# One program's order rewritten, and one tile's value products moved into it

## The reference, cut to what matters

```python
x = layernorm(x + L0_attn(x))   # latent attention, 32 heads, causal
x = layernorm(x + L0_ffn(x))    # routed low-rank stage, below
x = layernorm(x + L1_attn(x))   # q, k, v clipped; q and k normalised; ALiBi attention, 32 heads of 16
x = layernorm(x + L1_ffn(x))    # gated feed-forward, 1792 hidden

# L0_ffn: dense product, bias, and one of four low ranks chosen for each token
out = x @ W.T + b
probs = softmax(x @ gate_w.T + gate_b)          # the largest of four wins
final = (x @ A[:r].T @ B[:, :r].T)              # r = 8, 16, 32 or 64, by the winner
```

## Time and profile before

| | us |
|---|---|
| median of three runs | 1512.86 (1512.28 to 1513.26) |
| the profiled execution | 1512.49 |
| its span | 1510.7 |
| TensorE busy | 1422.4 (94%) |
| VectorE busy | 939.8 (62%) |
| ScalarE busy | 813.4 (54%) |
| GpSimd busy | 533.9 (35%) |

### The profile page before, as it was taken

One profiled execution on the slowest core, in us unless ns is written; L12 is line 12 of the kernel. 1 busy time (PEld: TensorE's weight loads), 2 busy tenths in 40 slices (PEclk: granted clock), 3 DMA queues, 4 the chain that ended last, 5 costly groups with the idle time before them and its releaser, 6 DMA issues. The chain is left out here.

```text
span 1510.7 us, 23933 instructions
## 1 busy us (share of the span) xinstructions
PE 1422.4 (94%) x8048; PEld 1011.7 (67%) x8048; DVE 939.8 (62%) x1521; ACT 813.4 (54%) x1731; POOL 533.9 (35%) x495
## 2 busy tenths in 40 slices
PE   5699999999999999999977987999999999999997
PEld 4566776776677777677646874555555558888885
DVE  4455665555566555566668646766666427767967
ACT  3566766666666566666533322565565665333433
POOL 0134454333445443344042134404131024444442
PEclk9799999999999999999989998999999999999998
DMA  5233334333333433332410045534335032000000
GB/s 186 71 47 47 41 50 53 36 48 44 45 41 51 53 35 48 42 40 38 87 56 1 1 56 71 71 44 62 53 53 107 34 118 120 1 0 1 3 25 28
DMA packets 61666, 75.90 MB, mean 50 GB/s; under 512 B 20641, under 2 KB 42145, under 8 KB 60705
## 3 DMA queue, kind: packets, MB, share of 16 engines
q1 hardware_dynamic: 57248, 64.55, 24.6%
q0 software_dynamic: 4352, 10.49, 5.1%
HBM read 42.49 MB, written 2.10 MB: 30 GB/s over the span
## 5 line engine op out<-in xcount | busy, mean ns | idle before, releaser
L1682 DVE TENSOR_REDUCE pm<-l_sm 128x2 f32<-128x1024 f32 (+1 forms) x192 | 178.5, 956 | 96.0 <-PE l_sm L1556 59.9
L1642 ACT ACTIVATE l_probs<-l_banks 128x512 f32<-128x512 f32 (+3 forms) x366 | 165.6, 495 | 134.1 <-PE l_banks L1586 83.0
L666 ACT ACTIVATE probs<-sc,nmax 128x128 f32<-128x128 f32 (+7 forms) x256 | 190.1, 743 | 72.1 <-DVE nmax L750 68.1
L750 DVE TENSOR_REDUCE nmax<-sc 128x1 f32<-128x128 f32 (+7 forms) x256 | 193.5, 756 | 32.6 <-PE sc L493 27.1
L674 ACT COPY pt<-tb 128x512 f32<-128x512 f32 (+3 forms) x256 | 129.3, 505 | 151.1 <-PE tb L507 150.1
L507 PE MATMUL tb<-ident,probs 128*128 128x128 f32 x1152 | 172.5, 275 | 2.1 <-ACT pt L674 1.1
L78 PE MATMUL sc<-k_h,q_h 128*128 128x512 f32 (+4 forms) x384 | 144.4, 376 | 10.5 <-DVE q_l L774 8.7
L507 PEld LDWEIGHTS tb<-ident,probs 128*128 128x128 f32 x1152 | 132.1, 141 | 13.5 <-DVE pt L758 3.8
L1583 PE MATMUL l_banks<-qk_bufs 128*128 128x512 f32 (+3 forms) x366 | 134.8, 410 | 0.8 <-ACT l_probs L1642 0.4
L529 PE MATMUL mb<-pt,ckv 128*64 128x512 f32 (+2 forms) x736 | 131.7, 493 | 3.2 <-DVE x_tok L740 2.9
L78 PE MATMUL sc<-k_h,q_l 128*128 128x512 f32 (+4 forms) x384 | 132.4, 345 | 0.0
(11 more groups left out here) (288 smaller groups left out, 3107.7 us busy)
## 6 DMA issues: line engine op xcount, KB each, us to landing
gated_late<-in_gated SPq DMA_DIRECT2D x11, 768.0 KB, 13.2
wout<-in_w_out SPq DMA_DIRECT2D x16, 512.0 KB, 4.4
late<-late SPq DMA_DIRECT2D x128, 64.0 KB, 2.0
rb<-rT SPq DMA_DIRECT2D x248, 32.0 KB, 4.5
qk_bufs<-late SPq DMA_DIRECT2D x96, 64.0 KB, 5.7
qk_bufs<-late POOLq DMA_DIRECT2D x96, 64.0 KB, 6.7
nope_t<-in_nope_by_dim SPq DMA_DIRECT2D x16, 192.0 KB, 3.9
late<-in_gated SPq DMA_DIRECT2D x3, 768.0 KB, 7.9
```

Source lines behind the costliest of these rows:

```text
L666: act.activation(prob_row(n, s), score_row(n)[0], ACT.Exp, bias=nmax[:, s:s + 1], accum_out=ssum[:, n:n + 1]).then_inc(exped, 1)
L750: dve.tensor_reduce(nmax[:, n % 4:n % 4 + 1], row, axes, ALU.max, negate=True).then_inc(negmax, 1)
L1642: act.activation(probs[(NC * g + c) % RING][:, h, 0:w], e_slot(g, n)[:, 0:w], ACT.Exp).then_inc(exped, 1)
L1682: dve.tensor_reduce(pm[g % 2][:, :, s, i, half], slot(("m", g, n))[:, :, 0:w], AX.X, ALU.max, negate=True).then_inc(freed, 1)
```

## The change

In the latent attention's tail VectorE takes no statistics of tiles 4 to 7; it takes them in the routed program, behind its first four lower halves. In the routed program the order of all four engines is another one, the eight bias additions move from GpSimd to VectorE in three places, and the value products of the last tile are computed there, behind the 16 projections, and copied out by VectorE. The ALiBi program computes 7 tiles of values, with half of the seventh ahead of the score units and half between the first two, and waits for 7. GpSimd there waits for the first maxima before it issues group 1's moves, and loads the constant rows of group 1 before that wait.

```diff
@@ stage_mla, tail_add
-                    dve.wait_ge(tail_read, j + 1)
-                    keep.n1.stats(dve, j, keep.x[:, j, :])
+                    if j < 4:
+                        dve.wait_ge(tail_read, j + 1)
+                        keep.n1.stats(dve, j, keep.x[:, j, :])
@@ stage_front, TensorE
+                def project_v(j):
+                    pe.wait_ge(wqh, 3 * DK)
+                    pe.wait_ge(wql, 3 * DK)
+                    pe.wait_ge(clip, len(order) - 3)
+                    first, rest = split_terms(cols(j), wqkv_h[2], wqkv_l[2])
+                    three(pe, po[0][:], first + rest).then_inc(qkv_ps, 1)
                 down_rank(0)
-                turn_x1(4)
-                turn_x1(5)
                 base(0)
                 back(0)
-                turn_x1(6)
-                turn_x1(7)
+                for j in range(4, ST):
+                    turn_x1(j)
                 base(1)
                 down_rank(1)
                 base(2)
+                back(1)
                 turn_lo(0)
-                back(1)
                 base(3)
-                turn_lo(1)
                 for j in range(4):
                     lora(j)
                 for j in range(4, ST):
                     base(j)
+                    if j == 4:
+                        turn_lo(1)
                     lora(j)
...
+                project_v(ST - 1)
@@ stage_front, ScalarE
                 upper_x(0, 0)
-                n1.root(act, 4, ST, 1)
                 upper_x(1, 1)
...
                 w_copy(3)
+                act.copy(b_hh[:], bT2).then_inc(w_h, 1)
+                n1.root(act, 4, ST, 1)
+                qkv_copy(0, range(2))
                 act.wait_ge(n1.inv_ok, 4)
                 for j in ON_ACT:
...
-                act.copy(b_hh[:], bT2).then_inc(w_h, 1)
                 ag_copy(0)
+                qkv_copy(0, range(2, DK))
                 for j in range(4, ST):
                     upper_x(j, j)
-                qkv_copy(0, range(DK))
-                qkv_copy(1, range(2))
+                qkv_copy(1, range(DK))
                 ag_copy(1)
                 upper_lo(0)
-                qkv_copy(1, range(2, DK))
+                n2.root(act, 0, 1, 0)
+                n2.root(act, 1, 2, 1)
+                normalise(0)
                 upper_lo(1)
-                n2.root(act, 0, 1, 0)
-                for j in range(1, 4):
+                for j in range(2, 4):
                     n2.root(act, j, j + 1, j)
                     normalise(j - 1)
@@ stage_front, VectorE
+                def add_bias(j):
+                    dve.wait_ge(tr_ps, j + 1)
+                    dve.tensor_tensor(keep.x[:, j, :], keep.x[:, j, :], bias, ALU.add).then_inc(biased, 1)
+
+                for j in range(4):
+                    lower_x(j, j)
+                for j in range(4, ST):
+                    n1.stats(dve, j, keep.x[:, j, :])
                 n1.variance(dve, 4, ST)
-                lower_x(0, 0)
                 n1.inverse(dve, 4, ST, 1)
                 dve.wait_ge(n1.inv_ok, 3)
-                lower_x(1, 1)
                 n1.normalise(dve, 4, keep.x[:, 4, :])
-                lower_x(2, 2)
                 n1.normalise(dve, 5, keep.x[:, 5, :])
-                for j in range(3, ST):
+                dve.wait_ge(keep.small_in, 16)
+                for j in range(2):
+                    add_bias(j)
+                for j in range(4, ST):
                     lower_x(j, j)
-                dve.wait_ge(keep.small_in, 16)
                 route(0)
+                for j in range(2, 4):
+                    add_bias(j)
                 lower_lo(0)
                 route(1)
+                add(0)
+                add(1)
+                n2.inverse(dve, 0, 1, 0)
                 lower_lo(1)
-                add(0)
-                for j in range(1, 4):
+                for j in range(2, 4):
                     add(j)
                     n2.inverse(dve, j - 1, j, j - 1)
                 n2.inverse(dve, 3, 4, 3)
+                for j in range(4, ST):
+                    add_bias(j)
...
+                dve.wait_ge(qkv_ps, len(order) + 1)
+                dve.tensor_copy(keep.v[:, ST - 1, :], po[0][:])
@@ stage_front, GpSimd
-                for j in range(ST):
-                    pool.wait_ge(tr_ps, j + 1)
-                    pool.tensor_tensor(keep.x[:, j, :], keep.x[:, j, :], bias, ALU.add).then_inc(biased, 1)
@@ alibi_order
-    order = [... cast ...] + [("v", k, j) for j in range(6) for k in range(DK)]
-    late_v = [("v", k, j) for j in (6, 7) for k in range(DK)]
+    order = [... cast ...] + [("v", k, j) for j in range(V_TILES - 1) for k in range(DK)]
+    late_v = [("v", k, V_TILES - 1) for k in range(DK)]
+    order += late_v[0:2]
     for n in range(M_HALF):
-        order += [("m", 0, n), late_v[n]]
+        order += [("m", 0, n)] + late_v[2 + n:3 + n]
@@ stage_alibi: SyncE before group 1's moves, TensorE before e(0, 0), GpSimd before values(0, 0)
-                wait for ST value tiles
+                wait for V_TILES = ST - 1 value tiles
@@ stage_alibi, GpSimd
-                for b in range(1, BUFS):
-                    pads(b)
-                    load_rows(b)
-                    if b == 1:
-                        move_keys(1)
-                        values(1, 1)
-                        pool.wait_ge(vx_ok, 2)
+                pads(1)
+                load_rows(1)
+                pool.wait_ge(rows_first, ROWS)
+                move_keys(1)
+                values(1, 1)
+                pool.wait_ge(vx_ok, 2)
+                pads(2)
+                load_rows(2)
```

More of the change, by code:

```diff
@@ L1320 @@
 AHEAD = 4
+V_TILES = ST - 1
 def chunk_cols(c):
@@ L1341, in alibi_order @@
 def alibi_order():
-    order = [("build", 0, 0), ("build", 0, 1), ("cast", 0, 0), ("cast", 0, 1)] + [("v", k, j) for j in range(6) for k in range(DK)]
-    late_v = [("v", k, j) for j in (6, 7) for k in range(DK)]
+    order = [("build", 0, 0), ("build", 0, 1), ("cast", 0, 0), ("cast", 0, 1)] + [("v", k, j) for j in range(V_TILES - 1) for k in range(DK)]
+    late_v = [("v", k, V_TILES - 1) for k in range(DK)]
+    order += late_v[0:2]
     for n in range(M_HALF):
-        order += [("m", 0, n), late_v[n]]
+        order += [("m", 0, n)] + late_v[2 + n:3 + n]
     order += [("top", 0, 0), ("m", 0, M_HALF), ("rows", 0, 0)]
@@ L1495, in _ @@
                 maxima(0, 0)
-                sp.wait_ge(vp, ST)
+                sp.wait_ge(vp, V_TILES)
                 move(sp, 1, 0, moved)
@@ L1572, in e @@
                         pe.wait_ge(rows_first, ROWS)
-                        pe.wait_ge(v_ev, ST)
+                        pe.wait_ge(v_ev, V_TILES)
                     if n == (0 if g else HG * C_HALF):
@@ L1769, in _ @@
                     pool.wait_ge(ones, PADS[0] + 2 * u + 2)
-                pool.wait_ge(v_ev, ST)
+                pool.wait_ge(v_ev, V_TILES)
                 values(0, 0)
                 pool.wait_ge(vx_ok, 1)
-                for b in range(1, BUFS):
-                    pads(b)
-                    load_rows(b)
-                    if b == 1:
-                        move_keys(1)
-                        values(1, 1)
-                        pool.wait_ge(vx_ok, 2)
+                pads(1)
[6 more added lines that the diff above has]
+                load_rows(2)
                 for g in range(GROUPS):
```

## The result

Four runs of the changed kernel gave a median of **1502.74 us** (1500.69 to 1504.59) beside 1512.57 us before: a ratio of 0.9937, with a 95% interval of 0.9926 to 0.9949. That is 9.8 us less, where I had forecast 15.9 less (1496.6). The time lies inside the range of 1491 to 1505 only because that reaches out to the rivals: the forecast's own 1493 to 1500 missed it. The profiled execution took 1504.59 us (span 1502.8), the slowest of the four, so the two traces differ by 7.9 us only.

What follows compares the result with a forecast made beforehand. TensorE was taken as busy over most of the span, so only its waits between 765 and 943 us could go. 3.5 + 5.2 + 7.2 = 15.9 from 1512.5 gave 1496.6 us; range 1493 to 1500, with rivals 1491 to 1505.

Steps and rivals of the forecast that it cites:

- GpSimd's chains: Rival, routed program: GpSimd's operations hold the moved bias additions until it runs dry, 6.4 us lost: 1503; chance 0.12.
- DMA-bound at m(1,0): Rival, ALiBi start: maxima queue behind load_rows(1), moves land as slowly as before, 5 of 7.2 us missing: 1501.6; chance 0.13.
- Tail, 3.5: End of the latent attention's program: without four statistics the next program starts at 768.9 instead of 772.36, 3.5 us earlier.
- Routed program, 5.2: Routed program: new engine orders bring project(0) to +52.1 instead of +57.2, 5.2 us, with project_v(7) costing nothing.
- to base(1): Routed program, stretch behind base(0): VectorE's moved work is covered by 1.9 us; base(1) starts at +15.5 instead of +17.05.
- Project_v(7): End of the routed program: 12 added matmuls, 2.73 us, fit before the boundary and cost nothing; uncovered 2.7.
- ALiBi start, 7.2: Start of the ALiBi program: m(1,0) 6.6 us earlier and a chain behind it some 0.6 us shorter, together 7.2.
- M(0,0) 0.95 sooner: ALiBi start: SyncE's moves start 1.0 us sooner, so the first score comes at 898.8 instead of 899.75.
- E(0,0) at +34.8: ALiBi start: the product for the first exponential, waiting for the maxima alone, taken at 913.5 instead of 915.45.
- the other bound: ALiBi start: E(0,0) at 915.5 if the maxima's 4 KB rows queue behind the 512 KB, against 912.9 otherwise.
- M(1,0) at +48.1: ALiBi start: m(1,0), needing tile work and all moves, taken at 926.8 between bounds 924 and 931, 6.6 us gained.
- better: Rival: clock never falls in the routed program's first 10 us (2 us) and moves land at 924 (1.5 us): 1493; chance 0.09.

Runs made afterwards that it cites:

- mended and filled: Changed kernel with GpSimd's added waits, group 0's rows before its zeros, group 1's behind the first maxima, plus unread products in TensorE's waits: 1500.27 us, ratio 0.9924.
- values back: Changed kernel with all eight value tiles and GpSimd's old order in the ALiBi program again, tail and routed order kept: 1506.10 us, ratio 0.9972.
- rows ahead: Changed kernel with GpSimd issuing the constant rows before clearing the pads in groups 0 and 1: 1501.80 us, ratio 0.9941.
- GpSimd later: Changed kernel with GpSimd waiting in the routed program for VectorE's first two bias additions and first routing masks before its weight halves: 1501.39 us, ratio 0.9934.
- same again: The changed kernel measured once more, nothing altered, six runs: 1503.00 us, ratio 0.9944 to the kernel before.

## Why the prediction was right in direction and too large by 6 us

- **Mechanisms.** The bound, the places and the names of the waits held: both boundaries, the masks, m(1,0). No rival took the place of the forecast. *GpSimd's chains* (6.4 us) came as 0.6 to 1.0; that the measured time is the 1503 of this rival is chance, for the missing 6 us are made of other things, listed here. Of *DMA-bound at m(1,0)* the first half came, the maxima that queue behind the rows; the wait at m(1,0) is gone.
- **Tail, 3.5**: measured 3.46 in the trace, and 3 to 4 in the time when the statistics go back.
- **Routed program, 5.2**: 1.9. (57.2 less 52.1 is 5.1; 5.2 is what was added up.) From base(4) on the step was exact (23.2 against 23.3, fast base(6)). Ahead of base(4) the forecast was 3.1 us short, and the step that failed is *to base(1)*: it started 2.1 us late, at +17.6, and took 0.8 longer at half clock; from there to base(4) all but 0.2 of the rest held. Read from the runs: with VectorE's first additions not held by GpSimd and full clock ("mended and filled") base(4) stands at 29.2, 0.3 off my sum; GpSimd adds 1.0 to it (30.25 with fillers and the old GpSimd order), and the slow base(1) of the first profile 1.7. I had put the fall of the clock into down_rank(0) and base(5), the latter as covered by VectorE, and that cover holds. But it falls at base(1) or base(6) too, by the profile, and there nothing covers it. In 7 of the 13 profiles with the new order this made project(0) 1.6 to 1.7 us later; the sum had no term for it.
- **Project_v(7)** cost nothing, as forecast: VectorE's copy (872.71, 0.69 us) ended ahead of ScalarE's last normalisation (874.01), and from project(0) to the boundary it is 49.1 us with these products and, in "values back", without them.
- **ALiBi start, 7.2**: 3.5, the largest error. *M(0,0) 0.95 sooner* failed: SyncE did start 1.3 us sooner, but the scores waited for a queue that held group 0's rows; with these issued first it is 1.6 sooner (and in one profile of eight it was so without that). *E(0,0) at +34.8* failed by 1.9: 1.1 of it is m(0,0), 0.7 the maxima behind group 1's rows. I had named that as the other bound and gone under the middle of the two. *M(1,0) at +48.1* came at +51.5 for the same reasons and a half clock from 905 to 915.5 (0.51); issuing group 0's rows first and group 1's behind the maxima gave +47.9 and, with GpSimd's waits, +48.1. The *better* rival's 1.5 us for moves that land at 924 had no ground in my own working: TensorE's order held m(1,0) to 926.3, 0.5 ahead of the forecast.
- **The page's rule.** The Trainium skill (SBUF — State Buffer, Who interferes with whom) says that of a VectorE instruction with two SBUF inputs and a GpSimd one that reads SBUF the second to be issued is blocked until the first is done. Here the trace agrees in length as well: a product of four numbers took 1.2 us, one GpSimd half 1.25. Of the two sums the one by that rule was the nearer in mechanism, since no addition took over 3 us (two took 3.45), and the 8.41 us of the earlier trace rows is left unexplained by it.
- **In the time.** TensorE's last latent product stood between 766.7 and 769.6 us in the 14 profiles, in no order with the kernels. So the 0.95 us is scatter of executions, ahead of anything that was changed; the medians differ by 9.8.

What stays open: why the clock falls at one of these places rather than another in a given run; and how much of the 6 us scatter between runs of one kernel it makes. Some 3 us can come from the latent programs by the numbers above, and the mean clock follows the times only partly (1498.58 us at 0.985, but 1502.17 at 0.978 and 1504.38 at 0.982).

## What to carry to other kernels

When work is moved off an engine, its queue moves up too: list what that engine will now issue earlier (here 512 KB of rows and 12 moves) and which small, urgent transfer it will be ahead of. Give such an engine a wait on the urgent event: without it the moved products gained nothing here. And where TensorE works in pieces, give the sum a term for a fall of its clock at a place that no other engine's list covers. Here 12 products in or partly in such a fall took 0.8 to 2.2 us more, and where nothing covered them project(0) came 1.6 to 1.7 us later.

## What the runs showed of the hardware

- A wait that ends on a DMA can be that of a small transfer behind a large one of another queue: the exponential that needs four DMAs of 4 KB started 2.5 to 2.8 us behind the end of their issue with 512 KB of rows in flight (six profiles, each ending a wait on these DMAs), 1.75 without the rows and without a wait, and 1.2 before the change and in "rows ahead", where the rows are issued 5 us sooner. The Trainium skill (DMA: Bandwidth & Descriptors, Queues, rings and completion order) says that a transfer's completion is written only after every earlier write of the same DMA engine, whichever queue it came by. The runs agree in direction; none shows the single engines.
- GpSimd's zeros, which read nothing, held VectorE's copies and casts of 16 to 32 numbers until they were done (up to 1.80 us instead of 0.18, and 0.75 instead of 0.17). The two-input additions of tiles 2 and 3 took 1.36 us for both at 793.87, as GpSimd finished, and 2.38 in "GpSimd later", where its halves began beside them.
- Both sides pay: four GpSimd halves took 6.21 us beside the bias additions and 4.99 alone.
- The order of instructions was the same in the profiles of "same again" and of the change, and the stretches at half clock were not: in the routed program 773 to 778, 786 to 789 and 810 to 813 in the change, 775 to 777 and 816 to 818 in "same again" (granted clock 0.50).
